# Gates by row tile, row norms finished together: the passage to the routing of a graph and expert network

## Chip, cores and metric

The kernel runs on one core of one Trainium2 chip. The metric is the device time of one execution in microseconds (us): before the change 2203.37 us, the median of 3 runs (2202.32 to 2203.42).

## What is computed

Four stages act on `x`, 1250 rows of 512, each on the row-normalized state and added to it: a graph layer, an expert layer with routing, a second graph layer, and a soft tree of eight experts. The change lies between the first two:

```python
h = relu(batch_norm(h @ W2 + b2, g2, be2))   # 1250 x 512, batch statistics over the rows
x = x + (layernorm(x) + h)                   # end of the first graph layer
y = layernorm(x)                             # row norms
gates = y @ gate_w                           # 1250 x 8
t = log(clip(gates, 1e-10))                  # Sinkhorn: 8 times columns, then rows
for _ in range(8):
    t = t - logsumexp(t, axis=-2); t = t - logsumexp(t, axis=-1)
# per expert: the 156 rows with the largest plan, routed = y[idx]; outputs = routed @ experts
# a chosen row counts where its plan is over 0.5; x = x + sum of its outputs / (times chosen + 1)
```

## The kernel before

Each engine has its own list of instructions, written out by hand, and the engines meet at semaphores. `v` is VectorE, `t` TensorE, `a` ScalarE, `q` GpSimd, `sp` the queue that issues DMAs. `s.mark` counts a VectorE step on a semaphore, `s.then` also waits for it, and a list can wait for such a count (`at.applied`, `at.planned`, `at.steps_made`).

The change is in `phase_route`. Rows stand in ten tiles of 125 (`NT`, `TR`). At its start `g.yT` holds the transposed graph output (four blocks of 128 features, `KD`, by 1250 rows) ahead of its batch norm. ScalarE applies scale, shift and relu to the columns of `BLOCKS` (418, 416, 416 columns), VectorE to two of the four feature blocks of the first 418. Then VectorE makes bf16 copies of five constants (`make_bf16`, L1163).

*Row tiles.* For each tile TensorE makes four transposes of `yT` into one of four PSUM banks (`produce`, L1041), and VectorE adds the bank to `x_rows` (L1185), takes the row statistics (L653), and finishes the norm of the tile two back: aggregation (L656), square root on ScalarE (L679), reciprocal (L644), shift (L646). ScalarE writes the normalized row tile to `c_rows` (L684), and `sp` stores it to DRAM (L1435). Between the tiles TensorE multiplies the stationary gate weights (8 columns) by 418 columns of `yT` (`gate_part`, L1311); ScalarE copies the 8-row results to `gT` (L1415), and ten transposes (L1319) bring the gates by row into bank 7. VectorE adds `gate_base`, scales by `rstd` and adds the shift's part (L1191, L1204 to L1208).

*Sinkhorn.* In each of 8 rounds VectorE sums columns (L1212), TensorE sums them over the partitions with a matrix of ones (L1342), VectorE divides, sums rows and divides (L1215 to L1220), and cuts half a piece of the expert weights (`cut_rest`, L1198), which waits for ScalarE's high part (`cut_w`, L1395). Behind the product TensorE makes one group of transposes of the adjacency `A1T` (`turn_tensor`, L1079 and L1081: pairs of blocks, up to 4 pairs, 18 groups in all), and ScalarE copies them back (`turn_scalar`, L1089 and L1092). One group stands ahead of the rounds, one behind them, eight in the search.

*Search.* The plan is copied sixteen times (`P16`, L1222), transposed in ten pieces (L1354), and a threshold for each expert is found in 8 rounds of counting (L1231 to L1239; TensorE L1360 and L1363). The chosen rows get places, and `token_of` drives GpSimd's gathers from the stored rows (L1582), which wait until all ten rows tiles are stored.

## Time and profile before

| | us |
|---|---|
| median of 3 runs | 2203.37 |
| profiled execution | 2205.09 |
| its span | 2203.3 |
| busy in the span: TensorE / VectorE / ScalarE / GpSimd | 2134.1 / 1544.1 / 1083.6 / 592.1 |
| granted TensorE clock, mean | 0.982 |

Busy time overlaps between engines. In the names of the profile PE is TensorE's products, PEld its weight loads, DVE VectorE, ACT ScalarE, POOL GpSimd, SPq the DMAs that `sp` issues. A row of the timeline gives start, duration, engine, line and operation, output from input with shapes, and in square brackets how long the engine had been idle and what ended that. A fp32 product stands as two MATMUL records, a transpose as one. A granted clock of 1.00 is TensorE's 2.4 GHz level, 0.50 its 1.2 GHz level.

### The profile page before, as it was taken

How to read it: one execution, taken by the hardware profiler on the slowest of the kernel's cores; microseconds unless marked ns; L12 is line 12 of the kernel's file. 1: busy time of each engine (PE TensorE's matmuls, PEld its weight loads, DVE VectorE, ACT ScalarE, POOL GpSimd, SP SyncE). 2: the span in 40 equal slices, each digit the busy share in tenths (PEclk: the TensorE clock that was granted, in tenths of full speed). 3: DMA queues.
4: the chain of work that ended last, by engine and by line, in shares of the span. 5: the costliest groups of instructions: out<-in, count | busy, mean ns of one | idle time of the engine just before them, and what ended most of it. 6: DMA issues, size and time to landing. Idle time of an engine off the chain costs nothing.

```text
span 2203.3 us, 30580 instructions
## 1 busy us (share of the span) xinstructions
PE 2134.1 (97%) x10662; PEld 1874.0 (85%) x10662; DVE 1544.1 (70%) x2664; ACT 1083.6 (49%) x2032; POOL 592.1 (27%) x1036
## 2 busy tenths in 40 slices
PE   8999985899999999999999999999999999999999
PEld 8999964597688888888888888888888888888888
DVE  8964575464876677777777776677777777776665
ACT  6952352453644454445554544454445555544453
POOL 4500001111133322223332233322223332233320
PEclk9999985999999999999999999999999999999999
DMA  2002022510111111111111111111111111111111
GB/s 66 2 10 68 1 87 84 160 33 30 34 48 39 44 39 39 39 62 39 39 39 44 48 48 44 39 39 39 46 56 39 39 44 39 48 53 39 39 39 57
DMA packets 71022, 101.35 MB, mean 46 GB/s; under 512 B 5847, under 2 KB 41255, under 8 KB 70871
## 3 DMA queue, kind: packets, MB, share of 16 engines
q1 hardware_dynamic: 67523, 93.70, 13.6%
q0 software_dynamic: 3040, 5.19, 0.8%
q8 instruction: 87, 1.43, 0.3%
q14 instruction: 64, 0.52, 0.1%
q10 hardware_dynamic: 308, 0.51, 0.1%
HBM read 91.63 MB, written 7.74 MB: 45 GB/s over the span
## 4 chain that ended last, share of the span: by engine, by line
PE 76%; DVE 0%; issue 0%; ACT 0%
PE psum L690 25%; PE psum L691 25%; PE psum L692 25%; PE psum L2345 1%; PE psum L2236 0%; PE psum L2226 0%; ACT w_forms_hi L2077 0%; ACT f_rows L684 0%; DVE x_rows L2525 0%; DVE stats L653 0%; PE psum L2243 0%; DVE norm_shift L646 0%; DVE x_rows L2492 0%; DVE hidden L2409 0%; ACT w_forms_hi L2075 0%
## 5 line engine op out<-in xcount | busy, mean ns | idle before, releaser
L690 PE MATMUL psum<-w_hi,hidden_hi 128*125 128x512 f32 x1280 | 503.9, 394 | 2.4 <-issue 2.4
L692 PE MATMUL psum<-w_hi,hidden_lo 128*125 128x512 f32 x1280 | 505.2, 395 | 0.0
L691 PE MATMUL psum<-w_lo,hidden_hi 128*125 128x512 f32 x1280 | 505.0, 395 | 0.0
L691 PE MATMUL psum<-x_forms_lo,w_forms_hi 128*128 128x418 f32 x1260 | 445.4, 353 | 0.0
L2492 DVE SCALAR_TENSOR_TENSOR x_rows<-psum,leaf_by_token,x_rows 125x512 f32<-125x512 f32 x320 | 234.0, 748 | 255.2 <-PE psum L692 255.2
L2018 POOL TENSOR_TENSOR w_forms<-w_raw 128x128 f32<-128x128 f32 x189 | 104.8, 583 | 1121.8 <-PE psum L692 579.5
L2116 ACT ACTIVATE hidden<-psum 128x418 f32<-128x418 f32 x315 | 162.0, 514 | 488.1 <-PE psum L692 485.9
L690 PEld LDWEIGHTS psum<-w_hi,hidden_hi 128*125 128x125 f32 x1280 | 237.8, 186 | 58.8 <-issue 2.7
L692 PEld LDWEIGHTS psum<-w_hi,hidden_lo 128*125 128x125 f32 x1280 | 237.1, 185 | 59.1
L691 PEld LDWEIGHTS psum<-w_lo,hidden_hi 128*125 128x125 f32 x1280 | 237.5, 186 | 54.4
L2465 DVE TENSOR_TENSOR hidden_lo<-hidden,hidden_hi 128x418 fp32r<-128x418 f32 (+1 forms) x384 | 255.2, 691 | 21.2 <-ACT hidden_hi L2138 21.2
L2128 ACT ACTIVATE hidden<-hidden,b1cols 128x414 f32<-128x414 f32 x315 | 201.5, 640 | 102.0 <-DVE hidden L2420 92.0
L691 PEld LDWEIGHTS psum<-x_forms_lo,w_forms_hi 128*128 128x128 f32 x1260 | 237.9, 189 | 7.7
L690 PE MATMUL psum<-x_forms_hi_late,w_forms_hi 128*128 128x418 f32 x630 | 224.1, 356 | 0.0
L690 PE MATMUL psum<-x_forms_hi_first,w_forms_hi 128*128 128x418 f32 x630 | 223.4, 355 | 0.7 <-DVE hidden L2409 0.7
L692 PE MATMUL psum<-x_forms_hi_first,w_forms_lo 128*128 128x418 f32 x630 | 222.1, 353 | 0.0
L692 PE MATMUL psum<-x_forms_hi_late,w_forms_lo 128*128 128x418 f32 x630 | 221.8, 352 | 0.0
L2018 POOL TENSOR_TENSOR w_forms<-w_raw,w_forms 128x128 f32<-128x128 f32 x378 | 220.1, 589 | 4.9
L2138 ACT ACTIVATE hidden_hi<-hidden 128x418 fp32r<-128x418 f32 (+1 forms) x384 | 204.2, 550 | 6.0
L2395 DVE TENSOR_TENSOR w_forms_lo<-w_forms,w_forms_hi 128x1792 fp32r<-128x1792 f32 x63 | 127.6, 2025 | 37.0 <-ACT w_forms_hi L2077 37.0
L2018 POOL TENSOR_TENSOR w_forms<-w_forms,w_raw 128x128 f32<-128x128 f32 x252 | 136.1, 540 | 4.9
L690 PEld LDWEIGHTS psum<-x_forms_hi_first,w_forms_hi 128*128 128x128 f32 x630 | 118.7, 188 | 8.6 <-DVE hidden L2409 1.0
(381 smaller groups left out, 3438.8 us busy)
## 6 DMA issues: line engine op xcount, KB each, us to landing
w_raw<-in_w SPq DMA_DIRECT2D x127, 512.0 KB, 3.7
expert_raw<-in_experts SPq DMA_DIRECT2D x8, 1024.0 KB, 5.8
expert_results_d<-expert_results SPq DMA_DIRECT2D x16, 160.0 KB, 4.8
c_rows_d<-c_rows SPq DMA_DIRECT2D x10, 250.0 KB
x_rows<-in_x SPq DMA_DIRECT2D x5, 448.0 KB
W_raw<-in_gnn_W SPq DMA_DIRECT2D x4, 512.0 KB, 4.4
W_raw<-in_gnn_W SPq DMA_DIRECT2D x1, 2048.0 KB, 9.4
b_by_token<-in_b SPq DMA_DIRECT2D x8, 256.0 KB, 3.8
```

The source lines that it names most:

```text
L690: t.matmul(out, stat[0], mov[0], start=start, stop=False, skip_group_check=again)
L691: t.matmul(out, stat[0], mov[1], start=False, stop=False, skip_group_check=again)
L692: return t.matmul(out, stat[1], mov[0], start=False, stop=stop, skip_group_check=again)
L2018: q.tensor_tensor(u[:, to, :], a, b, op).then_inc(w_sum, 1)
L2116: a.activation(slot_of(hid, G, b, j), g.psum[:, bank, 0:width(b)], ACT.Copy, scale=scale).then_inc(copied, 1)
L2128: a.activation(to, to, ACT.Gelu, bias=bias(G, j)).then_inc(active, 1)
L2138: a.activation(slot_of(hhi, G, b, j), slot_of(hid, G, b, j), ACT.Copy).then_inc(hi_cut, 1)
L2345: ins = t.matmul(g.psum[:, PLAIN_BANK[b][j], 0:hi - lo], g.wplain[:, k, j * 128:(j + 1) * 128], g.xf[:, k, lo:hi], start=k == 0, stop=k == ...
L2395: v.tensor_tensor(to[:, U1:U15 + 1, :], g.wsum[n % 2][:, U1:U15 + 1, :], of[:, U1:U15 + 1, :].bitcast(F32), ALU.subtract).then_inc(w_lo, 1)
L2465: v.tensor_tensor(slot_of(hlo, G, b, j), slot_of(hid, G, b, j), slot_of(hhi, G, b, j).bitcast(F32), ALU.subtract).then_inc(lo_cut, 1)
L2492: v.scalar_tensor_tensor(out=g.x_rows[:, i, :], in0=g.psum[0:TR, i % Y_BANKS, :], scalar=g.leaf[:, i, e:e + 1], in1=g.x_rows[:, i, :], op0 ...
```

## The change

- The first columns are worked on in two steps, 125 and 293 (`FIRST_COLUMNS`); the bf16 constants are made behind `P16`.
- Gates: `gate_part`, `gT` and its transposes go. For each row tile four products with the transposed block stationary and the gate weights moving write the gates by row (`gate_products`).
- Row norms: no finish in the tile loop. Square roots of nine tiles at once and of the last, then reciprocals, shifts and the gate arithmetic in the same split.
- Adjacency turns: three behind tiles 5, 7 and 9 (PSUM banks 4 and 5), seven in the Sinkhorn rounds 0 to 6, eight in the search as before. Two expert weight pieces are cut behind the first two turns.
- Rows for the store: normalized by ScalarE behind the Sinkhorn turns (three) and in the search rounds (seven); `sp` issues the third expert's load between the third and the fourth store.
- `P16` is made and awaited in halves, the digit products stand ahead of its last two transposes.

```diff
@@ -1060,20 +1060,23 @@
 TURNS = len(turn_groups())
-TURNS_IN_SINKHORN = SINKHORN + 2
+TURNS_IN_ROWS = 3
+TURNS_IN_SINKHORN = TURNS_IN_ROWS + SINKHORN - 1
...
 def turn_bank(i):
+    if i < TURNS_IN_ROWS:
+        return 4
...
     r, c0, n = turn_groups()[i]
-    if i >= TURNS_IN_SINKHORN:
+    if i >= TURNS_IN_SINKHORN or 1 <= i < TURNS_IN_ROWS:
         t.wait_ge(moved, 2 * i)
-    elif i >= 3:
+    elif i >= TURNS_IN_ROWS + 2:
@@ -1097,7 +1100,6 @@
     room = Room(nc, g.route_at)
-    gT = g.gT
@@ -1136,12 +1138,12 @@
     at.tried = [None] * len(SHIFTS)
+    FIRST_COLUMNS = ((0, TR), (TR, BLOCKS[0][1]))
+    ROWS_BEFORE_TURN = (5, 7, 9)
...
     normed = sem("c_normed")
-    gated = sem("r_gated")
-    copied = sem("r_copied")
@@ -1170,27 +1172,59 @@
             s = g.steps.on(v)
-            lo, hi = BLOCKS[0]
-            for d in range(KD // 2, KD):
-                at.scaled = s.mark(v.tensor_scalar(g.yT[:, d, lo:hi], g.yT[:, d, lo:hi], g.bn.scale[:, d:d + 1],
-                                                   g.bn.shift[:, d:d + 1], ALU.mult, ALU.add))
-            for d in range(KD // 2, KD):
-                s.wait(at.scaled - (KD - 1 - d))
-                at.applied = s.mark(v.tensor_scalar(g.yT[:, d, lo:hi], g.yT[:, d, lo:hi], 0.0, None, ALU.max))
-            make_bf16(v, s)
-            norm = NormSteps(v, s, g, stats)
-            for i in range(NT + NormSteps.LAG):
-                if i < NT:
-                    v.wait_ge(produced, i + 1)
-                    v.tensor_tensor(g.x_rows[:, i, :], g.x_rows[:, i, :], g.psum[0:TR, i % 4, :],
-                                    ALU.add).then_inc(added, 1)
-                    v.wait_ge(added, i + 1)
-                else:
-                    if i == NT + 1:
-                        v.wait_ge(moved, 1)
-                        s.mark(v.tensor_tensor(gates[:, :, :], g.gate_base[:, :, :],
-                                               g.psum[0:TR, 7, 0:NT * NE].rearrange("p (t e) -> p t e", t=NT), ALU.add))
-                norm.step(i)
+            at.applied = []
+            for lo, hi in FIRST_COLUMNS:
+                for d in range(KD // 2, KD):
+                    at.scaled = s.mark(v.tensor_scalar(g.yT[:, d, lo:hi], g.yT[:, d, lo:hi], g.bn.scale[:, d:d + 1],
+                                                       g.bn.shift[:, d:d + 1], ALU.mult, ALU.add))
+                for d in range(KD // 2, KD):
+                    s.wait(at.scaled - (KD - 1 - d))
+                    last = s.mark(v.tensor_scalar(g.yT[:, d, lo:hi], g.yT[:, d, lo:hi], 0.0, None, ALU.max))
+                at.applied.append(last)
+            stat = []
+            for i in range(NT):
+                v.wait_ge(produced, i + 1)
+                v.tensor_tensor(g.x_rows[:, i, :], g.x_rows[:, i, :], g.psum[0:TR, i % 4, :],
+                                ALU.add).then_inc(added, 1)
+                if i:
+                    s.wait(stat[i - 1])
+                    v.bn_aggr(g.meanvar[:, i - 1, :], g.stats[:, i - 1, :]).then_inc(stats.var, 1)
+                v.wait_ge(added, i + 1)
+                stat.append(s.mark(v.bn_stats(g.stats[:, i, :], g.x_rows[:, i, :])))
+            def inverse(lo, hi):
+                v.wait_ge(stats.dev, stats.after(hi - 1))
+                v.reciprocal(g.rstd[:, lo:hi], g.dev[:, lo:hi]).then_inc(stats.inverse, hi - lo)
+            def row_shift(lo, hi):
+                v.wait_ge(stats.inverse, stats.after(hi - 1))
+                v.scalar_tensor_tensor(out=g.shift[:, lo:hi], in0=g.meanvar[:, lo:hi, 0], scalar=-1.0,
+                                       in1=g.rstd[:, lo:hi], op0=ALU.mult, op1=ALU.mult).then_inc(stats.ready, hi - lo)
+            gate_sum = g.x_gates[:, NT * NE:(NT + 1) * NE]
+            E = NT - 1
+            early = [TR, E, NE]
+            inverse(0, E)
+            s.wait(stat[E])
+            v.bn_aggr(g.meanvar[:, E, :], g.stats[:, E, :]).then_inc(stats.var, 1)
+            row_shift(0, E)
+            v.wait_ge(moved, 1)
+            s.then(v.tensor_tensor(gates[:, :, :], g.gate_base[:, :, :],
+                                   g.psum[0:TR, 7, 0:NT * NE].rearrange("p (t e) -> p t e", t=NT), ALU.add))
+            at.scaled_gates = s.mark(v.tensor_tensor(
+                gates[:, 0:E, :], gates[:, 0:E, :], g.rstd[:, 0:E].unsqueeze(2).to_broadcast(early), ALU.mult))
+            v.wait_ge(stats.ready, stats.after(E - 1))
+            at.shifts = s.mark(v.tensor_tensor(gate_shift[:, 0:E, :], g.shift[:, 0:E].unsqueeze(2).to_broadcast(early),
+                                               gate_sum.unsqueeze(1).to_broadcast(early), ALU.mult))
+            inverse(E, NT)
+            s.wait(at.shifts)
+            s.mark(v.tensor_tensor(gates[:, 0:E, :], gates[:, 0:E, :], gate_shift[:, 0:E, :], ALU.add))
+            row_shift(E, NT)
+            at.scaled_gates = s.mark(v.tensor_scalar(gates[:, E, :], gates[:, E, :], g.rstd[:, E:NT], None, ALU.mult))
+            v.wait_ge(stats.ready, stats.after(E))
+            s.wait(at.scaled_gates)
+            s.then(v.scalar_tensor_tensor(out=gates[:, E, :], in0=gate_sum, scalar=g.shift[:, E:NT],
+                                          in1=gates[:, E, :], op0=ALU.mult, op1=ALU.add))
@@ -1198,14 +1232,6 @@
-            shape = [TR, NT, NE]
-            v.wait_ge(stats.ready, stats.after(NT - 1))
-            s.wait()
-            s.mark(v.tensor_tensor(gates[:, :, :], gates[:, :, :], g.rstd[:, :].unsqueeze(2).to_broadcast(shape),
-                                   ALU.mult))
-            s.then(v.tensor_tensor(gate_shift[:, :, :], g.shift[:, :].unsqueeze(2).to_broadcast(shape),
-                                   g.x_gates[:, NT * NE:(NT + 1) * NE].unsqueeze(1).to_broadcast(shape), ALU.mult))
-            s.then(v.tensor_tensor(gates[:, :, :], gates[:, :, :], gate_shift[:, :, :], ALU.add))
@@ -1219,9 +1245,12 @@
                                        ALU.mult))
-            at.planned = s.mark(v.tensor_copy(P16[:, :, :, :], plan[:, :, :].unsqueeze(3).to_broadcast(
-                [TR, NT, NE, 16])))
+            at.planned = []
+            for lo in (0, NT // 2):
+                at.planned.append(s.mark(v.tensor_copy(
+                    P16[:, lo:lo + NT // 2, :, :],
+                    plan[:, lo:lo + NT // 2, :].unsqueeze(3).to_broadcast([TR, NT // 2, NE, 16]))))
+            make_bf16(v, s)
@@ -1305,52 +1334,42 @@
         def _(t):
-            def gate_part(j):
-                b, d = divmod(j, KD)
-                lo, hi = BLOCKS[b]
-                ins = t.matmul(g.psum[0:NE, 4 + b, 0:hi - lo], g.gate[:, d, :], g.yT[:, d, lo:hi],
-                               start=d == 0, stop=d == KD - 1)
-                if d == KD - 1:
-                    ins.then_inc(gated, 1)
-            def gate_turn(b):
-                t.wait_ge(copied, b + 1)
-                for i in ((0, 1, 2), (3, 4, 5), (6, 7, 8, 9))[b]:
-                    ins = t.transpose(g.psum[0:TR, 7, i * NE:(i + 1) * NE], gT[:, i * TR:(i + 1) * TR],
-                                      g.ident[0:NE, 0:NE])
+            def gate_products(i):
+                for d in range(KD):
+                    ins = t.matmul(g.psum[0:TR, 7, i * NE:(i + 1) * NE], g.yT[:, d, i * TR:(i + 1) * TR],
+                                   g.gate[:, d, :], start=d == 0, stop=d == KD - 1)
...
             for i in range(NT):
-                if i == 0:
-                    t.wait_ge(g.steps.semaphore, at.applied)
-                    t.wait_ge(applied, 2)
+                if i < 2:
+                    t.wait_ge(g.steps.semaphore, at.applied[i])
+                    t.wait_ge(applied, KD // 2 * (i + 1))
                 elif i in (3, 6):
-                    t.wait_ge(applied, 2 + KD * (i // 3))
+                    t.wait_ge(applied, KD + KD * (i // 3))
...
                 produce(t, i, g.psum[0:TR, i % 4, :]).then_inc(produced, 1)
-                if 3 <= i < 9:
-                    gate_part(2 * i - 6)
-                    gate_part(2 * i - 5)
-            gate_turn(0)
-            gate_turn(1)
-            gate_turn(2).then_inc(moved, 1)
+                ins = gate_products(i)
+                if i in ROWS_BEFORE_TURN:
+                    turn_tensor(t, g, turned_a, moved_a, ROWS_BEFORE_TURN.index(i))
+            ins.then_inc(moved, 1)
             t.wait_ge(added, NT)
-            turn_tensor(t, g, turned_a, moved_a, 0)
...
                          stop=True).then_inc(moved, 1)
-                turn_tensor(t, g, turned_a, moved_a, 1 + i)
-            turn_tensor(t, g, turned_a, moved_a, 1 + SINKHORN)
-            t.wait_ge(g.steps.semaphore, at.steps_made)
-            for c in range(2):
-                t.matmul(g.psum[:, 7, 16 + c:17 + c], ident16[:, :],
-                         step16[:, DG_FIRST - DG_STEP + c:DG_FIRST - DG_STEP + c + 1], start=c == 0, stop=False,
-                         skip_group_check=True)
-            t.wait_ge(g.steps.semaphore, at.planned)
+                if i < SINKHORN - 1:
+                    turn_tensor(t, g, turned_a, moved_a, TURNS_IN_ROWS + i)
...
             for i in range(NT):
+                if i in (0, NT // 2):
+                    t.wait_ge(g.steps.semaphore, at.planned[i // (NT // 2)])
+                if i == NT - 2:
+                    t.wait_ge(g.steps.semaphore, at.steps_made)
+                    for c in range(2):
+                        t.matmul(g.psum[:, 7, 16 + c:17 + c], ident16[:, :],
+                                 step16[:, DG_FIRST - DG_STEP + c:DG_FIRST - DG_STEP + c + 1], start=c == 0,
+                                 stop=False, skip_group_check=True)
@@ -1385,38 +1404,46 @@
         def _(a):
-            def apply(b, d):
-                lo, hi = BLOCKS[b]
+            def apply(columns, d):
+                lo, hi = columns
...
                              scale=g.bn.scale[:, d:d + 1]).then_inc(applied, 1)
+            def deviations(lo, hi):
+                a.wait_ge(stats.var, stats.after(hi - 1))
+                a.activation(g.dev[:, lo:hi], g.meanvar[:, lo:hi, 1], ACT.Sqrt,
+                             bias=g.eps_col[0:TR, :]).then_inc(stats.dev, hi - lo)
+            def store_rows(t):
+                a.wait_ge(stats.ready, stats.after(t))
+                norm_rows(a, g, rows, t).then_inc(normed, 1)
...
-            for d in range(KD // 2):
-                apply(0, d)
-            for d in range(KD):
-                apply(1, d)
-            for i in range(NT + 2):
-                j = i - 2
-                if i < NT:
-                    deviation(a, g, stats, i)
-                if i in (1, 2):
-                    apply(2, 2 * i - 2)
-                    apply(2, 2 * i - 1)
-                if 0 <= j < NT:
-                    a.wait_ge(stats.ready, stats.after(j))
-                    norm_rows(a, g, rows, j).then_inc(normed, 1)
-                if i in (3, 5, 7):
-                    b = (i - 3) // 2
-                    lo, hi = BLOCKS[b]
-                    a.wait_ge(gated, b + 1)
-                    a.activation(gT[:, lo:hi], g.psum[0:NE, 4 + b, 0:hi - lo], ACT.Copy).then_inc(copied, 1)
-            for i in range(TURNS):
+            for columns in FIRST_COLUMNS:
+                for d in range(KD // 2):
+                    apply(columns, d)
+            for columns in BLOCKS[1:]:
+                for d in range(KD):
+                    apply(columns, d)
+            for i in range(TURNS_IN_ROWS):
                 turn_scalar(a, g, turned_a, moved_a, i)
-                if i < 2 * KD:
-                    cut_w(i // KD, i % KD)
+                if i < 2:
+                    cut_w(0, i)
+            deviations(0, NT - 1)
+            deviations(NT - 1, NT)
+            for i in range(SINKHORN - 1):
+                turn_scalar(a, g, turned_a, moved_a, TURNS_IN_ROWS + i)
+                if i < 2 * KD - 2:
+                    cut_w((i + 2) // KD, (i + 2) % KD)
+            for t in range(3):
+                store_rows(t)
+            for r in range(len(SHIFTS)):
+                turn_scalar(a, g, turned_a, moved_a, TURNS_IN_SINKHORN + r)
+                if 3 + r < NT:
+                    store_rows(3 + r)
@@ -1430,10 +1457,10 @@
             sp.dma_start(tables[:, :], g.consts_d[:, C_Q:C_END]).then_inc(tables_in, 16)
-            for t in range(NT):
-                sp.wait_ge(normed, t + 1)
-                sp.dma_start(g.c_d[t * TR:(t + 1) * TR, :], g.c_rows[:, t, :]).then_inc(g.c_stored, 16)
-            for e in range(2):
+            for e, of in ((0, range(3)), (1, range(3, NT))):
+                for t in of:
+                    sp.wait_ge(normed, t + 1)
+                    sp.dma_start(g.c_d[t * TR:(t + 1) * TR, :], g.c_rows[:, t, :]).then_inc(g.c_stored, 16)
@@ -2777,7 +2804,6 @@
         room = Room(nc, g.y_at + COLS)
-        g.gT = room("gates_T", [NE, N], F32)
```

## Rows read from the trace of the kernel before

**Rows 1.** The page, chain of work that ended last, shares of the span by engine.

```profile
PE 76%; DVE 0%; issue 0%; ACT 0%
```

**Rows 2.** Timeline (start us, duration us, engine, line, operation), start of the row tiles.

```profile
294.03 0.90 DVE L1175 TENSOR_SCALAR yT<-yT,bn_scale,bn_shift 128x418 f32<-128x418 f32 x2 [0.32 <-PEq L772]
...
294.85 0.66 DVE L1179 TENSOR_SCALAR yT<-yT 128x418 f32<-128x418 f32 x2
...
295.56 3.44 PE L1041 MATMUL psum<-small_consts,yT 128*125 128x128 f32 x16 [4.65 <-DVE yT L1179]
...
296.03 0.17 DVE L1167 CAST digit_steps_bf<-digits 128x10 bf16<-128x10 f32 x1
```

**Rows 3.** Timeline, two adds on VectorE, two row tiles on TensorE.

```profile
298.14 0.67 DVE L1185 TENSOR_TENSOR x_rows<-x_rows,psum 125x512 f32<-125x512 f32 x1
...
299.54 0.65 DVE L1185 TENSOR_TENSOR x_rows<-x_rows,psum 125x512 f32<-125x512 f32 x1
...
300.43 0.70 PE L1041 MATMUL psum<-small_consts,yT 128*125 128x128 f32 x4
...
302.56 0.70 PE L1041 MATMUL psum<-small_consts,yT 128*125 128x128 f32 x4
```

**Rows 4.** Stretches of TensorE: length, busy us (count), granted clock, DMA share, GB/s.

```profile
295.20:298.50 3.30, 2.94 (x14) 0.50 0.89 284
...
298.60:314.30 15.70, 15.55 (x70) 1.00 0.37 137
...
322.60:325.80 3.20, 3.20 (x14) 0.50 0.33 128
...
332.70:336.00 3.30, 3.30 (x17) 0.50 0.08 29
```

**Rows 5.** Timeline of TensorE, products with 8 moving columns, at either clock.

```profile
43.53 0.99 PE L522 MATMUL psum<-gate,x_T 128*125 128x8 f32 x8
...
44.38 0.54 PE L529 MATMUL psum<-column_onehot,low_onehot 125*128 125x140 bf16 x6
...
322.57 0.59 PE L1342 MATMUL psum<-colsum,small_consts 125*125 125x8 f32 x2 [0.67 <-DVE colsum L1212]
...
323.01 0.55 PE L1079 MATMUL psum<-small_consts,A1T 125*125 125x125 f32 x1
...
324.86 0.59 PE L1342 MATMUL psum<-colsum,small_consts 125*125 125x8 f32 x2
```

**Rows 6.** Timeline, last square root, first column sum, a turn's copies on ScalarE.

```profile
314.24 0.28 ACT L679 ACTIVATE dev<-meanvar,eps_col 125x1 f32<-125x1 f32 x1
...
315.89 0.29 DVE L1212 TENSOR_REDUCE colsum<-plan 125x8 f32<-125x80 f32 x1
...
321.94 0.38 ACT L1089 ACTIVATE A1T<-psum 125x250 f32<-125x250 f32 x1 [1.48 <-PE psum L1081]
...
322.62 0.62 ACT L1395 ACTIVATE expert_hi<-expert_raw 128x512 fp32r<-128x512 f32 x1
```

**Rows 7.** Timeline, Sinkhorn's first rounds: stored rows, first weight cut, next column sum.

```profile
314.43 2.21 ACT L684 ACTIVATE c_rows<-x_rows,norm_shift,rstd 125x512 f32<-125x512 f32 x3
...
317.62 0.62 ACT L1395 ACTIVATE expert_hi<-expert_raw 128x512 fp32r<-128x512 f32 x1
...
319.93 0.30 DVE L1212 TENSOR_REDUCE colsum<-plan 125x8 f32<-125x80 f32 x1
```

**Rows 8.** Timeline, from the finished plan to the first candidate.

```profile
335.96 0.83 DVE L1222 COPY plan_sixteen_times<-plan 125x1280 f32<-125x1280 f32 x1
...
338.62 1.26 PE L1354 MATMUL psum<-small_consts,plan_sixteen_times 125*128 125x125 f32 x10 [1.59 <-ACT A1T L1092]
...
339.92 0.16 DVE L1231 CAST candidate_bits<-psum 128x1 int32<-128x1 f32 x1 [3.13 <-PE psum L1354]
```

**Rows 9.** Timeline, a late copy in the search, first gather.

```profile
357.16 0.38 ACT L1092 ACTIVATE A1T<-psum 125x250 f32<-125x250 f32 x1
...
371.00 1.24 POOL L1582 DMA_INDIRECT rows_by_place<-c_rows_d,token_of_place  x1 [67.88 <-issue]
```

## Prediction

> **What bounds the kernel now.** The chain of work that ended last is 76% TensorE [rows 1], but it runs almost wholly in the later stages. The change touches 294 to 360 us, so I read that stretch by its timeline, in the order in which its parts release each other; what it does to the end is then a shift of everything behind it. Four parts lie in series: (a) the row tiles, 294.0 to 315.89, from the first batch-norm pass over yT to the first column sum of Sinkhorn; (b) eight Sinkhorn rounds to 335.96; (c) the way from the finished plan to the first candidate, 335.96 to 339.92 [rows 8]; (d) the search and the token list, which end in the first gather at 371.00 [rows 9].
>
> In (a) two engines are close to each other. VectorE's adds of two tiles lie 1.40 us apart where it does only the add, the statistics and their aggregation [rows 3]. TensorE's tiles lie 2.13 us apart (300.43 to 302.56 [rows 3]): four transposes and two gate products with 418 moving columns. It does this at the 2.4 GHz level: the granted clock is 0.50 from 295.2 to 298.5 and 1.00 from 298.6 to 314.3 [rows 4]. In (b) a round takes 2.29 us (322.57 to 324.86 [rows 5]), only the first takes 4.04 (315.89 to 319.93), because the first expert weights are cut at 317.62, behind ScalarE's stored rows and the first turn's copies [rows 6, 7].
>
> **The change, part by part.** I build the new course in absolute times of the profiled execution and compare the same points.
>
> *Start.* Only 125 of 418 columns are worked on before the first transposes. VectorE's four passes took 0.90 + 0.66 us for 418 columns [rows 2]; with 125 they take about 0.7 in all (the fixed 0.12 us of each stays). TensorE starts at about 294.8 instead of 295.56. The remaining 293 columns are done by about 295.9, behind which tile 1 waits no more, since tile 0's products run until then. The bf16 constants (up to 296.2 [rows 2]) leave this place.
>
> *Gate products.* Three blocks of four products, gate weights stationary (8 columns) and 418 columns moving, go. In come four products for each row tile with 125 columns of yT stationary and 8 moving: fp32 makes two passes of each, so eight passes with a weight load of 125 columns. This form is in the trace: eight passes took 0.85 us (43.53 to 44.38) at the full clock [rows 5]. At the half clock the column-sum product, 125 columns stationary, 8 moving, takes 0.44 us for its two passes (322.57 to 323.01 [rows 5]), so eight take 1.70 to 1.76. The Trainium skill ("TensorE: Matmul & The Clock Gate", LDWEIGHTS (loading the stationary operand)) says that a weight load costs by its columns and not by its rows; rows 5 agree, since the eight columns that move save nothing. The ten transposes of gates_T and their three ScalarE copies go too, at no gain on the path: TensorE and ScalarE do them between tiles.
>
> *Which clock.* This decides the case. Before, the level rose at 298.5, after sixteen 128-column transposes back to back since 295.56 (3.44 us for all [rows 2]). In the changed order tile 0's four transposes are followed by eight passes that move 8 columns, and so on for each tile. What the clock does with such a mix is shown in Sinkhorn: from 322.6 to 325.8 TensorE is busy in all of 3.20 us, with groups of eight wide transposes and narrow products between them, and stays at 0.50; it rises only after the stretch 332.7 to 336.0, where one narrow product stands among transposes [rows 4]. In the new mix eight narrow passes stand against four transposes, so it resembles the stretch without a rise, and is narrower still. So I take the 1.2 GHz level for all of part (a): the engine has been idle for more than 4 us when it starts [rows 2], after which the level was down before, and nothing takes it up.
>
> The Trainium skill (same page, Part 1: The HAM clock gate) says that the clock is set by how busy the engine has lately been, and that sustained matmul work releases it. Read on the busy row, that would give full clock; the row of 322.6 to 325.8, busy 3.20 of 3.20 us at 0.50, speaks against this reading. It is the second rival below.
>
> *Row tiles at 1.2 GHz.* A tile costs TensorE 16 transposes' 3.44 / 4 = 0.86, plus 1.70, together 2.56 (bounds 2.50 and 2.62). VectorE's 1.40 is hidden behind that. The first tile begins at 294.8 with the clock still up, so 2.2: to 297.0. Nine more: 23.0, to 320.0. Two adjacency turns of eight transposes now stand among the tiles (after tiles 5 and 7), 324.86 - 322.57 - 0.44 = 1.85 each [rows 5]: gates finished at 323.7.
>
> *Norms in one go, and the added wait.* ScalarE now does all square roots after the third turn's copies, and this turn (four transposes, 0.9) stands behind tile 9's gate products: turned at 324.7. The two copies hold ScalarE for 0.68 (321.94 to 322.62 [rows 6]), so the square roots start at about 325.4. Queued behind this wait are VectorE's reciprocal, the last aggregation, and the whole finish of the gates. From the last square root to the first column sum it was 1.65 us (314.24 to 315.89 [rows 6]); the new order has two more dependent steps of 0.27 and one small one, less the separate last tile: 2.25. First column sum at 327.7 instead of 315.89: +11.8. That the reciprocals and shifts leave VectorE's tile loop gives nothing here, for TensorE sets the pace.
>
> *Sinkhorn.* The two first weight cuts are done among the tiles, so round one takes 2.29 like the others: -1.75. The column-sum product comes ahead of a turn in seven rounds as before, 0.44 + 1.85 = 2.29, no more than VectorE's round; no change. The last round has no turn behind it.
>
> *Plan to candidate.* Before, the ten wide transposes began at 338.62, late behind ScalarE's copies of the last two turns, and took 1.26 at the full clock; candidate 3.96 us after 335.96 [rows 8]. Now no turn is left there, and the copy of the plan (0.83) comes in halves: first half at +0.47, ten transposes at 1.2 GHz 2.1, two digit products 0.2, drain and semaphore 0.3: 3.1. Gain 0.85 (1.6 at the full clock, where the moved constants, 0.8 behind the second half, become last). At the half clock the first search round has its eight transposes slower: +0.1.
>
> *Stored rows.* Ten normalizations (three took 2.21 us in a row [rows 7], one alone 0.8) move into the gap behind Sinkhorn's last copies (three) and into the search rounds (seven). There each shares its round with the copies of a turn; ScalarE is free after 357.16 + 0.38 in the sixth [rows 9]. I cost them at nothing: copies plus row are 2.0 us in rounds of 2.25 to 2.85. SyncE's queue now holds the third expert's load between store 3 and store 4, without a wait that matters. At 128 GB/s [rows 4] a store of 250 KB lands in 2 us, the last one some 8 us ahead of the gather that waits for it at 371.00 [rows 9]. Were that cover gone, the gather would wait for the rest.
>
> Sum: +11.8 - 1.75 - 0.85 + 0.1 = **+9.3 us**; I take +9.2. The profiled execution took 2205.09 us, 2203.3 of it span, 1.7 above the median 2203.37. The shift goes on the median: **2212.6 us**. Bounds: tile price 2.50 to 2.62 gives -0.5 to +0.6; the restarts of TensorE further down (after the gather, before the second graph stage) run some us at the half clock, longer or shorter by where the shift puts them, 1.5 to either side. Its own range is 2210.4 to 2215.
>
> **The rivals.**
>
> *Clock partly up.* The turns of eight wide transposes next to a tile's four lift the level for a while after tile 5 or 7. Each tile at 2.4 GHz costs 1.28 instead of 2.56, each turn 0.9 instead of 1.85. Two to four tiles so: 2.5 to 6 us less, 2205 to 2210. For it: the rise after 332.7 to 336.0 [rows 4]. Against: there one narrow product stood among transposes, here eight narrow passes follow at once on the twelve wide ones.
>
> *Clock up as before, not slower.* If the level rises near 298.6, TensorE needs 1.28 a tile and VectorE's 1.40 becomes the bound; with the two turns of 0.9 partly in the way tile 9's gates end near 311.6, the roots start near 313.1 and the column sum comes at 315.3: -0.5, then -1.75 and -0.85 to -1.6: about -3.5, **2199.9 us**. It decides from the point where the clock rises behind the first tiles; then nothing of the 11.8 is paid. For it: TensorE has no gap. Against: rows 4.
>
> *Late rows.* The gather waits for the last stores, or ScalarE's rows hold back a turn's copy and so a count: each round up to 0.5 later, 2 to 4 us on top: 2215 to 2217. Against it are the 8 us of cover.
>
> **How the numbers follow.** Half clock throughout 0.70; partly up 0.10; up as before 0.15; late rows 0.05. The likeliest gives 2212.6. The first two hold 0.80, so the range is 2205.0 to 2215.3. A measurement of this kernel can tell about 0.2% (4.4 us) from no change: slower means above 2207.8. Slower: 0.70 + 0.05 + half of the partly-up case, less a little of the first: 0.78. Same: the rest of partly-up and most of up-as-before: 0.17. Faster: 0.05.
>
> **What would show it.** Granted clock 0.50 from 295 to about 324 and row tiles 2.5 to 2.6 us apart on TensorE; gate passes 1.7 us a tile; first column sum near 327.7; eight rounds of 2.29; candidate 3.1 after the plan; the last stored row before the gather. A granted clock of 1.00 between 299 and 312 makes the forecast wrong by 12 us.

## The result, and the profile after the change

| | before | after |
|---|---|---|
| median of the runs, us | 2203.39 (2202.32 to 2203.68) | 2214.26 (2212.31 to 2214.97) |
| ratio, 95% interval | | 1.0045 [1.0033, 1.0057] |
| span of the profiled execution, us | 2203.3 | 2213.2 |
| first column sum of Sinkhorn starts | 315.89 | 327.79 |
| plan finished | 335.96 | 346.17 |
| first candidate | 339.92 | 349.29 |
| last bits of the threshold | 359.39 | 369.69 |
| first gather starts | 371.00 | 381.30 |

The changed kernel is slower by 0.45%. 2212.6 us, a loss of 9.2, had been forecast; the medians lie 10.9 apart, the two gathers 10.3, the two spans 9.9. A second set of runs on another chip gave 2214.2 against 2204.89, ratio 1.0039 [1.0024, 1.0053].

The timeline of the changed kernel at the row tiles, to be read beside rows 2 and 3:

```profile
294.67 1.19 PE L1041 MATMUL psum<-small_consts,yT 128*125 128x128 f32 x4 [4.11 <-DVE yT L1182]
...
299.73 1.20 PE L1041 MATMUL psum<-small_consts,yT 128*125 128x128 f32 x4
300.72 1.69 PE L1339 MATMUL psum<-gate,yT 128*125 128x8 f32 x8
300.96 0.69 DVE L1187 TENSOR_TENSOR x_rows<-x_rows,psum 125x512 f32<-125x512 f32 x1 [1.11 <-PE psum L1041]
...
309.86 0.55 PE L1082 MATMUL psum<-small_consts,A1T 125*125 125x125 f32 x1
311.68 1.06 PE L1041 MATMUL psum<-small_consts,yT 128*125 128x128 f32 x4
```

A tile takes TensorE four wide transposes (1.20) and eight passes over the gate weights (1.69, the next tile's transposes overlap their end); the adds of VectorE (L1187) follow every 2.53 us and each waits 1.11 or 1.12 us for TensorE. Where a turn of the adjacency stands between two tiles (309.86 to 311.68) the add waits 2.80. The windows of TensorE show the clock at which this is done; they are to be read beside rows 4:

```profile
295.20:298.50 3.30, 3.30 (x19) 0.50 0.88 317
299.00:307.00 8.00, 8.00 (x40) 0.50 0.28 106
307.00:323.00 16.00, 16.00 (x78) 0.50 0.00 1
```

TensorE is busy without a gap and the clock is at 0.50, 1.2 GHz, in all of it, where before it had been at 1.00 from 298.6 to 314.3 [rows 4]. In this profile it stays at 0.50 through Sinkhorn and the search, and is up again only at 393.4, 12 us behind the start of the gather. A second profile of the same kernel (a2_after, of the second set of runs) has the same 0.50 in all tiles and in the search, but in Sinkhorn its level was up for 3 us; the same stretch in both, a2_after first:

```profile
341.60:344.80 3.20, 1.43 (x10) 1.00 0.00 0
```

```profile
341.60:344.80 3.20, 2.96 (x13) 0.50 0.00 0
```

So the level in the tiles repeats, and the level further down is not the same in every run. The wait table of the changed kernel for the stretch from 293 to 330 us (engine, array and line of what waits, what it waits for; total us, times, longest) names what this costs, and the wait that the change adds:

```profile
DVE x_rows L1187 <- PE psum L1041: 13.6, 10, 2.8
DVE rstd L1197 <- ACT dev L1414: 2.2, 1, 2.2
```

The end of the row tiles' part, beside rows 6 and 7:

```profile
324.57 0.38 ACT L1092 ACTIVATE A1T<-psum 125x250 f32<-125x250 f32 x1 [4.18 <-PE psum L1084]
324.99 0.38 ACT L1095 ACTIVATE A1T<-psum 125x250 f32<-125x250 f32 x1
325.26 0.29 ACT L1414 ACTIVATE dev<-meanvar,eps_col 125x9 f32<-125x9 f32 x1
325.66 0.22 DVE L1197 RECIPROCAL rstd<-dev 125x9 f32<-125x9 f32 x1 [2.19 <-ACT dev L1414]
...
327.79 0.29 DVE L1238 TENSOR_REDUCE colsum<-plan 125x8 f32<-125x80 f32 x1
330.14 0.30 DVE L1238 TENSOR_REDUCE colsum<-plan 125x8 f32<-125x80 f32 x1
```

The third turn's two copies (L1092, L1095), then the square roots of nine tiles (L1414), then the reciprocal that waited 2.19 us for them: a plain series. The second column sum comes 2.35 us after the first; before it was 4.04 [rows 6, 7].

From the finished plan to the gather, beside rows 8 and 9:

```profile
346.17 0.90 DVE L1250 COPY plan_sixteen_times<-plan 125x640 f32<-125x640 f32 x2
349.29 0.16 DVE L1260 CAST candidate_bits<-psum 128x1 int32<-128x1 f32 x1 [1.54 <-PE psum L1373]
349.56 0.55 PE L1082 MATMUL psum<-small_consts,A1T 125*125 125x125 f32 x1
...
352.88 0.57 PE L1082 MATMUL psum<-small_consts,A1T 125*125 125x125 f32 x1 [0.83 <-ACT A1T L1095]
...
354.15 0.16 DVE L1260 CAST candidate_bits<-psum 128x1 int32<-128x1 f32 x1 [0.20 <-PE psum L1382]
...
354.97 0.57 PE L1082 MATMUL psum<-small_consts,A1T 125*125 125x125 f32 x1 [0.41 <-ACT A1T L1095]
356.80 0.21 PE L1382 MATMUL psum<-enough,groups_bf 128*128 128x1 bf16 x1
...
368.57 0.25 SPq L1463 DMA_DIRECT2D c_rows_d<-c_rows  x1
369.69 0.16 DVE L1272 CAST threshold_low_bits<-psum 128x1 int32<-128x1 f32 x1
381.30 1.24 POOL L1609 DMA_INDIRECT rows_by_place<-c_rows_d,token_of_place  x1 [78.96 <-issue]
```

The candidate comes 3.12 us after the plan (3.96 before [rows 8]). The last store of rows is issued at 368.57, 12.7 us ahead of the gather. What the rows in the middle say about the search is told further down.

### The profile page after: what moved, and what is told of

The parts are those of the page before. It is cut to its first block, busy times and chain, and to the rows that moved or that the text cites. A ratio compares the mean times of both kernels' runs of the same rounds, so it can differ in the third digit from the quotient of the medians.

```text
span 2213.2 us, 30659 instructions
## 1 busy us (share of the span) xinstructions
PE 2146.4 (97%) x10708; PEld 1893.8 (86%) x10708; DVE 1541.4 (70%) x2655; ACT 1081.0 (49%) x2023; POOL 592.3 (27%) x1036
## 4 chain that ended last, share of the span: by engine, by line
PE 75%; DVE 0%; ACT 0%; DMA 0%; issue 0%
PE psum L690 25%; PE psum L691 25%; PE psum L692 24%; PE psum L2372 1%; PE psum L2263 0%; PE psum L2253 0%; DMA w_raw<-in_w 0%; DVE w_lo L2427 0%; ACT w_forms_hi L2104 0%; PE psum L2270 0%; ACT w_hi L2113 0%; DVE x_rows L2519 0%; ACT f_rows L684 0%; DVE x_rows L2552 0%; DVE stats L653 0%
```

## The experiments

The theory: the whole loss is one thing, the level of TensorE's clock in the row tiles; the level stays down because the gate products move 8 columns behind a wide weight load, and the rest of the change gains 2.5 us. Rivals: the new order of work (turns between tiles, square roots last, stored rows among the search rounds) costs the time by itself; or the level is down because TensorE stood idle ahead of the tiles, whatever stands in them. The columns "column sum" and "gather" below are the starts of these two instructions in each kernel's profile.

| kernel | ratio to before, 95% | median us | column sum | gather |
|---|---|---|---|---|
| before | 1 | 2203.39 | 315.89 | 371.00 |
| after | 1.0045 [1.0033, 1.0057] | 2214.26 | 327.79 | 381.30 |
| after, second set | 1.0039 [1.0024, 1.0053] | 2214.20 | 327.35 | 380.47 |
| e1_gates_128 | 0.9989 [0.9979, 0.9999] | 2200.91 | 314.44 | 367.10 |
| e2_gates_64 | 1.0020 [1.0010, 1.0030] | 2206.97 | 322.33 | 374.54 |
| e3_warm | 1.0006 [0.9994, 1.0019] | 2207.22 | 321.43 | 374.53 |
| e4_roots_first | 1.0031 [1.0020, 1.0043] | 2210.28 | 325.17 | 377.81 |
| e6_before_narrow | 1.0046 [1.0029, 1.0063] | 2213.16 | 322.42 | 377.44 |
| e7_128_roots | 0.9984 [0.9974, 0.9994] | 2200.72 | 313.83 | 365.58 |
| e5_128_warm_roots | 0.9968 [0.9957, 0.9980] | 2197.43 | 311.74 | 363.32 |
| e8_sums_128 | 0.9982 [0.9972, 0.9991] | 2200.27 | 312.51 | 366.72 |
| e10_warm_roots_narrow | 0.9999 [0.9989, 1.0010] | 2205.00 | 312.15 | 365.67 |
| e9_filled | 0.9962 [0.9948, 0.9976] | 2196.02 | 311.30 | 362.67 |

The kernels below "after" ran on three chips, each with its own runs of the kernel before (medians 2203.65 for e1 to e4, 2204.35 for e5 to e8, 2204.89 for the second set, e9 and e10), so kernels of different groups are compared by their ratios. All kernels compute the whole reference; where products are added, nothing reads them.

### Gate products that move 128 columns

The order of the changed kernel is kept; only the moving operand of the gate products becomes the eight gate columns repeated sixteen times. Fifteen of the sixteen copies fall on columns of the bank that are written again later or not read.

```diff
-  ins = t.matmul(g.psum[0:TR, 7, i * NE:(i + 1) * NE], g.yT[:, d, i * TR:(i + 1) * TR],
-                 g.gate[:, d, :], start=d == 0, stop=d == KD - 1)
+  ins = t.matmul(g.psum[0:TR, 7, i * NE:(i + 16) * NE].rearrange("p (w e) -> p w e", w=16),
+                 g.yT[:, d, i * TR:(i + 1) * TR],
+                 g.gate[:, d, :].unsqueeze(1).to_broadcast([128, 16, NE]),
+                 start=d == 0, stop=d == KD - 1)
```

> The changed kernel, but each gate product moves 128 columns (the 8 gate columns sixteen times over) instead of 8; outputs are the same. The weight loads, the number of passes and all waits stay. Theory 'clock' (the passes that move 8 columns leave TensorE at 1.2 GHz, and that makes the row tiles 2.5 us long): a pass is bounded by its weight load either way, so a tile is no longer at a given level, but the level rises near 299 us; tiles then 1.4 us apart, first column sum near 315, and 2200 us (2198 to 2202). Rival 'passes' (the weight loads of 125 columns set the tile's length, the clock only goes with it): no change, 2214 us.

Measured: 2200.91 us, ratio 0.9989 [0.9979, 0.9999]. Windows of TensorE and its timeline in this kernel:

```profile
295.20:298.50 3.30, 3.30 (x23) 0.71 0.97 354
299.00:307.00 8.00, 8.00 (x76) 1.00 0.23 86
```

```profile
298.31 0.60 PE L1041 MATMUL psum<-small_consts,yT 128*125 128x128 f32 x4
...
299.63 0.60 PE L1041 MATMUL psum<-small_consts,yT 128*125 128x128 f32 x4
...
314.44 0.29 DVE L1238 TENSOR_REDUCE colsum<-plan 125x8 f32<-125x80 f32 x1
```

Sixteen times the columns, and the loss is gone: the clock rises at 297.1, within the second tile (0.71 is the mean of the window), a tile then takes 1.32 us (298.31 to 299.63), the column sum comes 13.4 us earlier than in the changed kernel and the gather 14.2. Of the 14.2, 0.85 is the search, told further down. Nothing else differs between the two kernels, so the order of the work doesn't cost the 10.9 us; with the level up it gains (371.00 to 367.10 against before).

### Gate products that move 64 columns

The same edit with eight copies in place of sixteen.

```diff
-  ins = t.matmul(g.psum[0:TR, 7, i * NE:(i + 1) * NE], g.yT[:, d, i * TR:(i + 1) * TR],
-                 g.gate[:, d, :], start=d == 0, stop=d == KD - 1)
+  ins = t.matmul(g.psum[0:TR, 7, i * NE:(i + 8) * NE].rearrange("p (w e) -> p w e", w=8),
+                 g.yT[:, d, i * TR:(i + 1) * TR],
+                 g.gate[:, d, :].unsqueeze(1).to_broadcast([128, 8, NE]),
+                 start=d == 0, stop=d == KD - 1)
```

> The changed kernel with 64 moving columns in each gate product (the gate columns eight times over). Theory 'clock': I can't say from the rows whether 64 is enough to bring the level up; if it is, 2200 as with 128, if not 2214; a time between means that it comes up late or goes down again. I lean to 2214. Rival 'passes': 2214.

Measured: 2206.97 us, ratio 1.0020 [1.0010, 1.0030]: between the two, nearer to neither. The value to which I leaned was the one without a rise. The windows:

```profile
299.00:307.00 8.00, 8.00 (x39) 0.50 0.21 78
313.60:320.00 6.40, 5.48 (x49) 0.99 0.00 0
```

The level does rise, but late, near 313.7, with seven of ten tiles done. So the width has not two outcomes but three: up at 297.1 with 128 columns, up at 313.7 with 64, not up among the tiles with 8. The moment is that of one profile: three of the ten times lie at 2210.56 to 2211.39, where the level may have risen later still; none of these was profiled.

### Products ahead of the tiles, gate products narrow

Fifteen products of the identity with itself fill TensorE's idle time ahead of the tiles; the gate products stay as in the changed kernel.

```diff
+ t.wait_ge(m2_drained, 2 * KD)
+ for i in range(11):
+     t.matmul(g.psum[:, 0, 0:128], g.ident, g.ident, start=True, stop=True)
...
+ for i in range(4):
+     t.matmul(g.psum[:, 3, 0:128], g.ident, g.ident, start=True, stop=True)
```

> The changed kernel with fifteen additional products of the identity with itself (128 moving columns, result never read) in the idle time of TensorE ahead of the row tiles, so that the level is 2.4 GHz when the first tile starts. Rival 'idle before' (the level was lost in the idle time and nothing else, so that with a warm start the tiles run at full clock): tiles 1.4 us apart throughout, 2199 us. Theory 'clock': it starts at 1.00 and falls within the first tiles, because passes that move 8 columns don't hold it; one to three tiles gain 1.2 us each: 2211 to 2213 us.

Measured: median 2207.22 us, but the ten times lie in two groups: 2199.32, 2200.34, 2200.50, 2202.15 and 2206.84 to 2209.47 (six). The profile is of one of the second group:

```profile
299.00:307.00 8.00, 8.00 (x50) 0.62 0.26 98
301.50:320.00 18.50, 16.67 (x80) 0.50 0.00 0
```

```profile
300.16 0.94 PE L1342 MATMUL psum<-gate,yT 128*125 128x8 f32 x8
...
301.95 1.69 PE L1342 MATMUL psum<-gate,yT 128*125 128x8 f32 x8
```

The first tiles run at 1.00 and TensorE has no gap, yet at 300.9 the level falls (0.62 is the mean of the window), and the same passes take 1.69 instead of 0.94. Neither number that had been set (2199 for idle time alone, 2211 to 2213 for the clock) is the median. Both accounts were half right: the idle time ahead of the tiles does matter (with it gone, five tiles run at 2.4 GHz in the profile and four runs of ten come out near 2200), and the mix of narrow passes does not reliably hold the level.

### Square roots ahead of the third turn's copies

The wait that the change adds, taken by itself: ScalarE makes the square roots before the third turn instead of behind it.

```diff
-  for i in range(TURNS_IN_ROWS):
+  for i in range(TURNS_IN_ROWS - 1):
...
+  turn_scalar(a, g, turned_a, moved_a, TURNS_IN_ROWS - 1)
```

> The changed kernel, but ScalarE takes the square roots ahead of the copies of the third turn, not behind them. It measures the wait that the change adds: VectorE stood idle 2.19 us ahead of the first reciprocal. Theory: the reciprocal starts behind the last statistics, near 323.4 instead of 325.66, and the column sum 2 us earlier: 2212.2 us. Rival: the column sum then waits for the third turn's transposes or copies, nothing gained: 2214.3.

Measured: 2210.28 us, ratio 1.0031 [1.0020, 1.0043]. Its timeline (VectorE, the last tile's add and the first column sum):

```profile
321.72 0.69 DVE L1187 TENSOR_TENSOR x_rows<-x_rows,psum 125x512 f32<-125x512 f32 x1 [1.12 <-PE psum L1041]
325.17 0.29 DVE L1238 TENSOR_REDUCE colsum<-plan 125x8 f32<-125x80 f32 x1
```

From the last add to the column sum it is 3.45 us; in the changed kernel it is 5.73 (322.06 to 327.79). So the wait costs 2.28, close to the 2.19 for which the reciprocal stood; the other 0.34 by which the column sum is earlier was there at the first add. The wait is real, but it is a fifth of the loss, and the tiles stay 2.53 apart and at 0.50. The median lies 1.9 below the 2212.2 expected. In the profile the gather comes 3.49 earlier than in the changed kernel, and the part that is neither this wait nor the first add is the search, 19.54 instead of 20.40: the level was up from 348.2 to 351.8, and no run shows that the square roots brought that about.

### One part alone: the kernel before, with the narrow gate products

Into the kernel before goes only the new form of the gate products; its norms, turns, stored rows and constants stay.

```diff
- if 3 <= i < 9:
-     gate_part(2 * i - 6)
-     gate_part(2 * i - 5)
+ ins = gate_products(i)     # four products: yT columns of tile i stationary, 8 gate columns moving
...
- gate_turn(0)
- gate_turn(1)
- gate_turn(2).then_inc(moved, 1)
+ ins.then_inc(moved, 1)
```

> The kernel before with one part of the change alone: the gates by row tile from products that move 8 columns. Theory 'clock': the level stays at 1.2 GHz, tiles 2.53 us apart from 295.56, first column sum at 323.5 instead of 315.89 (+7.6), the first round's stall a little shorter (1.4 instead of 1.75), the ten transposes of the plan and the first search rounds slower by 1 us: 2203.65 + 8 = 2211.7 us (2210 to 2213). Rival 'the rest of the change costs it' (the turns among the tiles, the late roots): no more than 2205.

Measured: 2213.16 us, ratio 1.0046 [1.0029, 1.0063].

```profile
298.60:314.30 15.70, 15.70 (x76) 0.50 0.25 86
```

```profile
298.07 0.69 DVE L1185 TENSOR_TENSOR x_rows<-x_rows,psum 125x512 f32<-125x512 f32 x1 [1.11 <-PE psum L1041]
300.60 0.69 DVE L1185 TENSOR_TENSOR x_rows<-x_rows,psum 125x512 f32<-125x512 f32 x1 [1.03 <-PE psum L1041]
...
322.42 0.30 DVE L1212 TENSOR_REDUCE colsum<-plan 125x8 f32<-125x80 f32 x1
326.46 0.30 DVE L1212 TENSOR_REDUCE colsum<-plan 125x8 f32<-125x80 f32 x1
```

The level doesn't rise among the tiles and the adds are 2.53 apart, as in the changed kernel, although none of the rest of the change is there. (It rises later, at 333.6 in Sinkhorn.) This edit changes two things at once: the gate products are narrow, and they stand behind every tile from the first, where the kernel before has sixteen transposes in a row ahead of its first gate product [rows 2]. Narrow products that begin only behind the fourth tile were not run; what the width does by itself is shown by e1. The column sum comes at 322.42, 6.5 us later than before (323.5 had been expected), and the first round still takes 4.04 (0.35 less had been expected). In its profile the gather moves by 6.4 us; its four times spread from 2208.64 to 2216.62, so the size of this part is known only to the interval, the sign is not in doubt.

### Both repairs, and more

Wide gate products together with the square roots first:

```diff
-                 g.gate[:, d, :], start=d == 0, stop=d == KD - 1)
...
+                 g.gate[:, d, :].unsqueeze(1).to_broadcast([128, 16, NE]),
+                 start=d == 0, stop=d == KD - 1)
...
-  for i in range(TURNS_IN_ROWS):
+  for i in range(TURNS_IN_ROWS - 1):
```

> The changed kernel with 128 moving columns in the gate products and the square roots ahead of the third turn's copies. Tiles 1.3 us apart as with 128 columns alone, and the roots 2 us earlier; both are in series: 2200.9 - 2 = 2198.9 us. Rival: with the clock up the third turn takes only 0.9 us, so the roots gain 1 us or less: 2200.

Measured: ratio 0.9984 [0.9974, 0.9994], gather 365.58, 1.5 us ahead of e1. From the last add to the column sum it is 3.44 us (310.39 to 313.83), in e1 4.53 (309.91 to 314.44): with the level up the third turn is short, and moving the square roots past it gives 1.1 us instead of 2.3. That is the rival's account, and the median 2200.72 is the rival's 2200; the intervals of e7 and e1 (0.9979 to 0.9999) overlap, so the gain is seen in the profiles and not in the times. In e7 the level rose at 298.9, in the third tile, and in e1 at 297.1: with wide products too the moment differs from run to run.

The same with the fifteen products ahead of the tiles:

```diff
+ t.wait_ge(m2_drained, 2 * KD)
+ for i in range(11):
+     t.matmul(g.psum[:, 0, 0:128], g.ident, g.ident, start=True, stop=True)
...
+ for i in range(4):
+     t.matmul(g.psum[:, 3, 0:128], g.ident, g.ident, start=True, stop=True)
```

> As the one before, with the fifteen additional products in the idle time ahead of the tiles. The first two tiles no longer run at 1.2 GHz: first tile's gap of 2.2 becomes 1.3, and all tiles at 1.3: 1.0 us less than without them, 2197.8 us; and less spread than the warm start alone had (2199 to 2209), because wide passes hold the level.

Measured: 2197.43 us, ratio 0.9968 [0.9957, 0.9980]; all tiles at 1.00, column sum 311.74. It came within half a microsecond of the expectation. The level fell at 313.2, and was up again from 323.4 to 330, where the last three rounds of Sinkhorn take 2.08 or 2.09 us.

Then, to keep the level up in Sinkhorn, its column-sum product made 128 columns wide as well:

```diff
-                t.matmul(g.psum[0:TR, 6, 0:NE], g.ones[0:TR, 0:TR], colsum[:, :], start=True,
+                t.matmul(g.psum[0:TR, 6, 0:16 * NE].rearrange("p (w e) -> p w e", w=16), g.ones[0:TR, 0:TR],
+                         colsum[:, :].unsqueeze(1).to_broadcast([TR, 16, NE]), start=True,
                          stop=True).then_inc(moved, 1)
```

> As the one before, and the column-sum products of the Sinkhorn rounds move 128 columns too (the 8 sums sixteen times over). Theory: the level stays at 2.4 GHz through the rounds, which then take 2.08 us instead of 2.29 (as two rounds of the warm kernel at full clock did): -1.5, and the first search rounds keep it for a while, -0.5: 2195.8 us. Rival: the idle time between roots and first round takes the level down before the rounds, and the rounds' gaps keep it down: 2197.8.

Measured: 2200.27 us, ratio 0.9982 [0.9972, 0.9991], 3 us more than without it; 2195.8, or 2197.8 by the rival, had been expected. The timeline of TensorE:

```profile
315.11 0.77 PE L1366 MATMUL psum<-colsum,small_consts 125*125 125x128 f32 x2 [0.83 <-DVE colsum L1241]
```

The product lies between two steps of VectorE, so its duration is on the path of the round; at the half clock it takes 0.77 where the narrow one takes 0.59, and the rounds at that level are 2.47 to 2.50 instead of 2.29. The level fell at 315.1 all the same; TensorE had waited 0.83 us for VectorE in this round. The same widening that costs a tile nothing costs a round 0.2 us. In the two profiles that explains less than half of the loss: of the 3.40 by which the gather comes later than in e5, the eight rounds hold 1.50, the way to the candidate 0.28 and the search 0.84 (20.39 instead of 19.55, with the level down in it); 0.77 stood before the first column sum, where the two kernels are the same.

The other way to fill the gap, seven identity products between the third turn and the first round, where nothing waits for them:

```diff
  ins.then_inc(moved, 1)
  t.wait_ge(added, NT)
+ for i in range(7):
+     t.matmul(g.psum[:, 0, 0:128], g.ident, g.ident, start=True, stop=True)
```

> The fastest kernel so far (128 columns, warm start, early roots) with seven more identity products in TensorE's idle time between the third turn and the first Sinkhorn round. Theory: the level, which fell at 313.5 in that idle time, holds for some rounds more, each then 2.08 instead of 2.29: 0.5 to 1.5 us less, 2196.4. Rival: TensorE's gaps within the rounds take it down anyway: 2197.4.

Measured: 2196.02 us, ratio 0.9962 [0.9948, 0.9976].

```profile
311.30 0.29 DVE L1241 TENSOR_REDUCE colsum<-plan 125x8 f32<-125x80 f32 x1
313.38 0.30 DVE L1241 TENSOR_REDUCE colsum<-plan 125x8 f32<-125x80 f32 x1
...
317.55 0.30 DVE L1241 TENSOR_REDUCE colsum<-plan 125x8 f32<-125x80 f32 x1
319.85 0.30 DVE L1241 TENSOR_REDUCE colsum<-plan 125x8 f32<-125x80 f32 x1
```

Three rounds take 2.08 us; the level falls at 316.3, and the fourth to the seventh take 2.29. This is the version with the lowest median: 0.38% below the kernel before, and it keeps the whole change that by itself cost 0.45%. That the seven products gain anything over e5 is not shown: the intervals of the two overlap (0.9957 to 0.9980 for e5), and in the profiles the eight rounds take 17.50 instead of 17.57, since e5 had its fast rounds at the end.

### Narrow passes with everything else repaired

The kernel of e5 with 8 moving columns again, to separate the width from the idle time ahead:

```diff
-                 g.gate[:, d, :].unsqueeze(1).to_broadcast([128, 16, NE]),
-                 start=d == 0, stop=d == KD - 1)
...
+                 g.gate[:, d, :], start=d == 0, stop=d == KD - 1)
```

> Warm start and early roots with the products of the change as they are (8 moving columns): all of the fastest kernel so far but the wide products. If the tiles with 8 moving columns can hold the level in some runs, as the spread of the warm kernel (2199 to 2209) suggests, this one has two groups, near 2198 and near 2206; if they never hold it, one group near 2205. The fastest kernel so far had 2197.4 with 128 columns, so the difference to it is the price of the narrow form with everything else equal: 8 us where the level falls, 0 where it holds.

Measured: median 2205.00 us, ten times from 2198.03 to 2208.64 (three below 2201, seven from 2204.4 up). The profile is of a run of 2200.83:

```profile
299.00:307.00 8.00, 8.00 (x76) 1.00 0.28 105
```

```profile
298.37 0.68 PE L1044 MATMUL psum<-small_consts,yT 128*125 128x128 f32 x4
...
299.68 0.68 PE L1044 MATMUL psum<-small_consts,yT 128*125 128x128 f32 x4
```

Here the narrow mix runs at 1.00 through all ten tiles (until 310.7), 1.31 us a tile. So the width is not needed for the speed of a tile, nor does a narrow mix take the level down every time. From the times I infer that it does so in most runs, at a moment that differs: seven of ten lie over 2204, while e5, the same with wide products, has all its seven between 2195.12 and 2198.46. No slow run of e10 was profiled. Even this profile, whose tiles cost nothing more, has its gather 2.35 us later than e5: the level is down from 310.7 to the gather, which costs 0.81 in Sinkhorn, 0.28 up to the candidate and 0.85 in the search. The difference of 0 that was expected where the level holds in the tiles was too small by that. What decides in which run the level is held is not settled by these runs.

## Why the prediction was right, and where it was off

**The level of the clock.** The step that decided was the reading of rows 4 and 5 together: a stretch with TensorE busy in all of it and the level at 0.50, with narrow products among transposes. The changed kernel repeats it (8.00 of 8.00 and 16.00 of 16.00 us busy, clock 0.50), and e1 shows that the level is what costs the time: 128 columns in place of 8 take the loss away. e6, with narrow products behind every tile of the kernel before, shows the same loss there. The Trainium skill ("TensorE: Matmul & The Clock Gate", Part 1: The HAM clock gate) says that the clock is set by how busy the engine has been of late; by the busy share that the profile prints the trace does not agree, for it is full in the changed kernel at 0.50 and full in e1 at 1.00.

That the forecast came true was in part luck, because the row it leaned on doesn't decide. The stretch from 322.6 to 325.8 showed transposes and narrow products at 0.50 in one profile; later profiles show the same Sinkhorn work with the level rising in it, in e2 at 327.4, in e6 at 333.6, in e5 at 323.4, and in one profile of the changed kernel itself (341.3) but not in the other. One stretch of rows was a sign and no more; that the new mix, with eight narrow passes a tile, stays down was known only when it ran.

**The price of a tile.** Forecast 2.56 (2.50 to 2.62), measured 2.53; a turn 1.85, measured 1.82 (309.86 to 311.68). Rows 5 bear out that moving only 8 columns saves nothing; whether a weight load costs by its columns or by its rows they can't tell, since this load has 125 of the one and 128 of the other. The first tile was taken at the full clock (2.2); the level was down from 294.6 and it took 2.52 (294.67 to 297.19). That and the other small misses cancel: third turn forecast at 323.7, begun at 323.35; square roots 325.4, begun at 325.26; from there to the column sum 2.25, measured 2.53. Column sum forecast at 327.7, measured 327.79: +11.9 where +11.8 was written.

**The added wait.** It stands where the prediction put it, in series behind the third turn. e4 puts 2.3 us on it at the half clock, e7 1.1 at the full one; the prediction had it inside its sum, without a price for it alone.

**Sinkhorn and the candidate.** Eight rounds 18.38 instead of 20.07: -1.69 (forecast -1.75, all of it in the first: 2.35 against 4.04). Plan to candidate 3.12 (forecast 3.1): -0.84.

**The search: the term that was mis-sized.** +0.1 was written, for the first round's transposes at the half clock. From candidate to last bits it took 20.40 instead of 19.47: +0.93. The first three rounds take 2.36, 2.50 and 2.93 us; before they took 2.24, 2.25 and 2.36. All turns of the search pass through one pair of banks, so a turn starts only when ScalarE has copied the one before. In the changed kernel (fence above) the first turn of the search starts at 349.56 and runs at the half clock; the second starts at 352.88 and the third at 354.97, each released by ScalarE's copy of the one before (in brackets), the third 0.82 us behind its own candidate (354.15). The group product of that round (356.80) is queued behind it on TensorE. e2 has the same order of turns, but its level rises in the first turn (transposes of 0.55, then of 0.27); its timeline in the same place:

```profile
343.73 0.55 PE L1082 MATMUL psum<-small_consts,A1T 125*125 125x125 f32 x1
344.62 0.27 PE L1082 MATMUL psum<-small_consts,A1T 125*125 125x125 f32 x1
...
346.52 0.37 PE L1082 MATMUL psum<-small_consts,A1T 125*125 125x125 f32 x1 [0.41 <-ACT A1T L1095]
...
347.96 0.16 DVE L1260 CAST candidate_bits<-psum 128x1 int32<-128x1 f32 x1
348.23 0.55 PE L1082 MATMUL psum<-small_consts,A1T 125*125 125x125 f32 x1
```

The third turn follows its candidate after 0.27, the three rounds take 2.25, 2.24 and 2.36, and the search 19.46, as before. e10, whose level is down there, takes 20.40 like the changed kernel. All thirteen profiles fall into two groups in this way: 20.39 or 20.40 in the five whose level is down through the search (the two of the changed kernel, e3, e8, e10), and 19.46 to 19.55 in the eight whose level is up for a part of the first three rounds. e4 is among the eight, with the turns, the stored rows and the 8 columns of the changed kernel. So neither the moved rows nor the other numbering of the turns cost the 0.9; the half clock does. The prediction looked at the round in which the slower work lies and not at who takes over the same banks two rounds later.

**Stored rows.** Nothing, as forecast: the last store is issued at 368.57, and the gather keeps its distance of 11.61 us from the last bits of the threshold (359.39 to 371.00, 369.69 to 381.30). e2 with its 19.46 us shows the search carrying seven of these rows at no cost.

**Sum and rest.** 11.90 - 1.69 - 0.84 + 0.93 = 10.3 up to the gather; from the gather to the end 1831.9 instead of 1832.3, -0.4, within the 1.5 to either side that was kept for the restarts. In the other kernels this last length lies between 1829.4 and 1833.5, so a difference of 2 us between two kernels' single profiles says nothing; the start of the gather is the better measure. Against the forecast of +9.2 for the median, 0.8 of the 1.7 that it missed is the search; the rest is less than the interval of the ratio, 1.0033 to 1.0057 or 7.3 to 12.6 us.

**The rivals.** *Clock partly up* did not happen in the changed kernel: neither turn among the tiles lifted the level (windows above). It is what e2 does, for another reason, and its time, 2206.97, lies in that rival's range of 2205 to 2210. (2.5 to 6 us less than 2212.6 would be 2206.6 to 2210.1; and the forecast's own bounds add up to 2210.6 and 2214.7, not 2210.4 and 2215. Both slips are small and nothing hangs on them.) *Clock up as before* was 2199.9; e1 is that case made true and gives 2200.91, column sum forecast 315.3, measured 314.44. *Late rows*: the last store is issued 12.7 us ahead of the gather; less the 2 us that the prediction reckoned for its landing, that is some 10.7 of cover where 8 were reckoned. The 0.70 against 0.15 between the level down and the level up was worth more doubt than I gave it in one respect: e3 and e10 show that the same mix can run at either level, depending on how it is entered.

## What to carry to other kernels

Before small products with a wide weight load replace wide ones, find stretches of the same mix in the trace, in more than one profile, and read their granted clock: the cheaper work left the engine at 1.2 GHz here, and a tile took 2.53 us instead of 1.32. Where such products hide between other work, repeat the moving columns to 128: here it cost nothing a tile (1.32 us against 1.31) and gave 12 us back (ratio 1.0045 to 0.9989); where they lie on a dependent path, it costs their longer duration (0.59 to 0.77 us). When a stage is slowed, follow its buffers, not only its engine: the turn that came late was two rounds behind the one that was slow.

## What the runs showed of the hardware that I had not expected

The level of TensorE's clock did not follow the busy time of the profile's rows. With weight loads of 125 columns and 8, 64 or 128 moving columns a group of eight passes took 1.69, 1.78 and 1.92 us at 1.2 GHz, so the load sets the pace and the columns hardly count; yet after some 4 us of idle time the level was up at 297.1 or 298.9 with 128 (e1, e7), at 313.7 with 64 (e2), and in no tile with 8 (both profiles of the changed kernel, e4, e6).

With 8 columns the level was held until 300.9 (e3) or through all tiles (e10, until 310.7) when it was up at the start, and was lost in most of the runs: ten times of one kernel from 2199.32 to 2209.47, ten of the other from 2198.03 to 2208.64, where the changed kernel's nine lie between 2212.28 and 2214.97. A kernel that stands on such an edge has no one time, and a single profile of it shows one of two courses.
